# First mixture-of-experts stage of a two-layer decoder: expert weights loaded during the attention in front of it, residual sum of X and normalised X on ScalarE, list products at other places

## The reference

```python
x = x + _L0_xattn_ref(_layernorm(x), ctx_1024, ctx_1024)      # attention in front, "a0"
x = x + _L0_ffn_ref(_layernorm(x), ...)                       # first feed-forward stage, "f0"

def _L0_ffn_ref(x, centroids, routing_bias, Wfc_r, Wproj_r, Wfc_sh, Wproj_sh):   # x is normalised
    raw = einsum('bsd,ed->bse', x, centroids)
    _, top_idx = top_k(sigmoid(raw + routing_bias), 2)         # 2 of 8 routed experts per token
    combine = ...                                              # softmax of the two scores
    shared_out = sum over 2 shared experts of gelu(x @ Wfc_sh.T) @ Wproj_sh.T
    routed_out = sum over 8 experts of combine * (gelu(x @ Wfc_r.T) @ Wproj_r.T)
    return x + shared_out + routed_out
```

## Time and profile before

| what | us |
|---|---|
| median of three runs | 1243.5 (1243.29 to 1244.32) |
| the profiled execution's own time | 1240.97 |
| its span, from the first to the last instruction | 1239.2 |
| PE busy in the span | 1114.3 (90%) |
| DVE busy | 818.9 (66%) |
| ACT busy | 636.0 (51%) |
| POOL busy | 596.2 (48%) |

### The profile page before, as it was taken

How to read it: one execution, slowest core, us unless ns; L and a number is a source line. 1 busy time by engine, 2 the same in 40 slices (tenths; PEclk the granted TensorE clock), 3 DMA queues, 4 the chain that set the end, 5 groups by cost and what they waited for, 6 DMA issues and landing times. The chain is left out here.

```text
span 1239.2 us, 31324 instructions
## 1 busy us (share of the span) xinstructions
PE 1114.3 (90%) x11494; PEld 937.7 (76%) x11494; DVE 818.9 (66%) x1784; ACT 636.0 (51%) x1143; POOL 596.2 (48%) x608
## 2 busy tenths in 40 slices
PE   6989998999999999399999999996899978899970
PEld 4766666679999977288888888885577668899970
DVE  6768997853322443368888888885588867566762
ACT  5416774534566543066666666663678720366640
POOL 4772233315666575634334444442334324677775
PEclk9999998899999999799999999998999969899995
DMA  7001221502233321100000000000011060133342
GB/s 199 10 2 34 71 51 38 208 5 57 69 79 78 91 82 38 40 2 2 0 0 0 0 0 0 0 1 1 19 19 19 8 228 12 53 88 85 86 128 63
DMA packets 59537, 60.78 MB, mean 49 GB/s; under 512 B 12241, under 2 KB 48721, under 8 KB 58929
## 3 DMA queue, kind: packets, MB, share of 16 engines
q1 hardware_dynamic: 49904, 41.63, 11.3%
q0 software_dynamic: 8640, 17.71, 5.6%
q10 hardware_dynamic: 896, 0.17, 0.1%
HBM read 41.77 MB, written 15.60 MB: 46 GB/s over the span
## 5 line engine op out<-in xcount | busy, mean ns | idle before, releaser
L1629 POOL DMA_INDIRECT f_xn<-f_xn_rows,f_source x142 | 138.1, 972 | 41.9 <-issue 40.7
L2012 PE MATMUL f_bank<-f_xT,f_w_tile 128*128 128x128 f32 x1136 | 152.1, 277 | 0.0
L2023 PE MATMUL f_bank<-f_w_down,f_hidden 128*128 x1136 | 150.4, 276 | 0.0
L2012 PEld LDWEIGHTS f_bank<-f_xT,f_w_tile 128*128 128x128 f32 x1136 | 140.5, 194 | 0.0
L2023 PEld LDWEIGHTS f_bank<-f_w_down,f_hidden 128*128 128x128 f32 x1136 | 138.9, 193 | 0.0
L1050 POOL TENSOR_TENSOR ret_rstd<-ret_var,ret_minus_half 128x8 f32<-128x8 f32 x32 | 52.7, 1647 | 173.3 <-DVE ret_var L1089 173.3
L1640 POOL DMA_INDIRECT f_hot_row<-f_slots_y,f_slots x112 | 108.6, 970 | 33.5 <-issue 32.9
L885 PEld LDWEIGHTS a_mixed_psum<-a_v_diag,a_probT 128*64 128x64 f32 x2048 | 66.6, 139 | 59.9 <-ACT a_probT L837 43.7
L747 POOL TENSOR_TENSOR X<-X,a_mixed 128x128 f32<-128x128 f32 x64 | 29.2, 457 | 158.0 <-DVE a_mixed L780 154.6
L1904 ACT ACTIVATE f_w_tile<-f_w_up 128x512 f32 x142 | 87.6, 620 | 28.9 <-DVE f_owner L1809 26.8
L788 DVE TENSOR_REDUCE a_top<-a_scores 128x16 f32<-128x1024 f32 x64 | 78.3, 1224 | 34.2 <-PE a_scores L870 33.3
(11 more groups left out here) (302 smaller groups left out, 2797.5 us busy)
## 6 DMA issues: line engine op xcount, KB each, us to landing
f_slots_y<-f_y_out SPq DMA_DIRECT2D x70, 128.0 KB, 2.3
a_v_rows<-in_ctx SPq DMA_DIRECT2D x16, 256.0 KB, 4.0
f_xn_rows<-f_xn SPq DMA_DIRECT2D x16, 256.0 KB, 13.3
f_w_up<-in_f_up SPq DMA_DIRECT2D x1, 2560.0 KB, 9.8
f_w_down<-in_f_down SPq DMA_DIRECT2D x1, 2560.0 KB, 17.1
f_xn<-f_xn_rows,f_source POOLq DMA_INDIRECT x142, 2.6
X<-in_x SPq DMA_DIRECT2D x4, 512.0 KB, 6.2
kv_ctxT<-in_ctxT SPq DMA_DIRECT2D x8, 256.0 KB, 5.6
```

Of the source, the lines that this page charges most:

```text
L1629: pool.indirect_dma_start(out=x_in[:, s % RING, :], out_offset=None, in_=xn_rows[:, :], in_offset=bass.IndirectOffsetOnAxis(ap=source[:, s ...
L2012: last = pe.matmul(bank_h[m % 3][:, j * P:(j + 1) * P], w_tile[m % W_RING][:, j * P:(j + 1) * P], xT[m % 3][:], start=True, stop=True)
L2023: last = pe.matmul(bank_y[m % 2][:, 0:D].unsqueeze(1), hidden[m % 3][:, j, :], w_down[:, bass.ds(expert + E0, 1), j, :], start=(j == 0), s ...
```

## The change

Three parts, all of them in f0 and the attention a0 in front of it.

1. The weight arrays get a fixed place at the top of SBUF (class `HeldWeights`), and SP starts their two loads as the first instructions of the attention block a0, ahead of a0's own loads of keys and values for the third and later groups. f0 no longer loads them; its engines wait on the new semaphore.
2. POOL's eight additions X + xn are gone. ACT does them, as X * (1 + rstd) + (-mean * rstd), one instruction per tile with a scale and a bias per token, eight tiles after each of the first four shared units. DVE makes the two small operands `x_scale` and `x_shift` behind the last tile of xn. The first gather no longer waits for X + xn, and DVE's additions of shared results count the new semaphore in tiles.
3. The table `COLLECT` puts list products 0 to 4 at other places among the shared units.

```diff
+class HeldWeights:
...
+    def sync(self, sp):
+        for dst, src in ((self.w_up, self.up), (self.w_down, self.down)):
+            sp.dma_start(dst[:], self.g.dram[src]).then_inc(self.loaded, 16)
...
             @block.sync
             def _(sp):
+                if held:
+                    held.sync(sp)
                 for j in range(setup.early, 2):
...
-                if spec["plus_xn"]:
-                    for q in range(GROUPS):
-                        pool.wait_ge(S["xn_ready"], GTILES * (q + 1))
-                        x = g.X[:, GTILES * q:GTILES * (q + 1), :]
-                        pool.tensor_tensor(x, x, xn[:, GTILES * q:GTILES * (q + 1), :], ALU.add)\
-                            .then_inc(S["xn_added"], 1)
...
+                if spec["plus_xn"]:
+                    dve.scalar_tensor_tensor(out=x_shift[:], in0=g.mean[:], scalar=-1.0, in1=g.rstd[:],
+                                             op0=ALU.mult, op1=ALU.mult).then_inc(S["scale_ready"], 1)
+                    dve.tensor_scalar(x_scale[:], g.rstd[:], 1.0, None, ALU.add).then_inc(S["scale_ready"], 1)
...
                     def weights(unit):
+                        if unit < TILES // PLUS_TILES:
+                            act.wait_ge(S["scale_ready"], 2)
+                            act.wait_ge(S["xn_ready"], TILES)
+                            for s in range(PLUS_TILES * unit, PLUS_TILES * (unit + 1)):
+                                nc.scalar.activation(g.X[:, s, :], g.X[:, s, :], ACT.Identity, bias=x_shift[:, s:s + 1],
+                                                     scale=x_scale[:, s:s + 1]).then_inc(S["xn_added"], 1)
...
-                pe.wait_ge(S["weights_loaded"], 16 * len(weight_loads))
+                wait_for_weights(pe)
                 if shared:
-                    COLLECT = {(3, "up"): (0,), (3, "down"): (1,), (4, "up"): (2, 3), (4, "down"): (4, 5),
-                               (5, "up"): (6,), (5, "down"): (7,)}
+                    COLLECT = {(3, "down"): (0, 1), (4, "up"): (2,), (4, "down"): (3, 4)}
```

More of the change, by code:

```diff
@@ L717, in attention @@
         statistics = RowStatistics(g, name, ctx)
+        assert not held or g.nc.sbuf_base <= held.begin
         with nc.Block() as block:
@@ L1457, in ffn_phase @@
         pair, slots = sb("weights", [P, TOP_K, TILES]), sb("slots", [P, TOP_K, TILES], I32)
-        w_up, w_down = sb("w_up", [D, E, FFN]), sb("w_down", [P, E, FT, D])
+        held_weights = spec["held"]
+        if held_weights:
+            w_up, w_down = held_weights.w_up, held_weights.w_down
+        else:
+            w_up, w_down = sb("w_up", [D, E, FFN]), sb("w_down", [P, E, FT, D])
         owner, source = sb("owner", [1, M], I32), sb("source", [P, M], I32)
@@ L1510, in ffn_phase @@
         rows = [h[:].rearrange("p n t d -> p t n d") for h in row_sets]
+        assert not held_weights or nc.sbuf_base <= held_weights.begin
         bank = g.banks(name, ctx)
@@ L1533, in ffn_phase, with wait_for_weights @@
         loads = [(gate_w[:], dram[spec["gate_w"]]), (gate_b[:], dram[spec["gate_b"]].to_broadcast([P, EXPERTS])),
[L1534 removed]
+                 (rank[:], dram["rank"]), (before[:], dram["before"]),
+                 (tile_numbers[:], dram["tile_numbers"]), (segment_table[:], dram["segment_table"]), (row_numbers[:], dram["row_numbers"]),
                  (token_rows[:], dram["token_rows"])]
         n_loads = len(loads)
[L1537 removed]
+        def wait_for_weights(eng):
+            if held_weights:
+                eng.wait_ge(held_weights.loaded, 16 * 2)
+            else:
+                eng.wait_ge(S["weights_loaded"], 16 * len(weight_loads))
+        weight_loads = [] if held_weights else [(w_up[:], dram[spec["w_up"]]), (w_down[:], dram[spec["w_down"]])]
         if biased:
@@ L2033, with ffn0 @@
 WARM_START, WARM_COUNT, WARM_BETWEEN, WARM_UP = 28, 120, 6, 24
-def ffn0(g, weights):
-    ffn_phase(g, "f0", dict(kind="sigmoid", plus_xn=True, part_tiles=(20, 12), last=False, shared=2, following=weights, added_at=(65,), hot_later=(4, 10, 16), listed=16, ahead=(8, 13), more_rows=0, gelu=ACT.Gelu, gate_w="f0_gate_w",
-                            gate_b="L0_ffn_routing_bias", w_up="f0_up", w_down="f0_down", b_up=None))
+def ffn0(g, weights, held):
+    ffn_phase(g, "f0", dict(kind="sigmoid", plus_xn=True, part_tiles=(20, 12), last=False, shared=2, following=weights, held=held, added_at=(65,), hot_later=(4, 10, 16), listed=16, ahead=(8, 13), more_rows=0, gelu=ACT.Gelu, gate_w="f0_gate_w",
+                            gate_b="L0_ffn_routing_bias", b_up=None))
 def ffn1(g):
-    ffn_phase(g, "f1", dict(kind="softmax", plus_xn=False, part_tiles=(16, 8, 8), last=True, shared=0, following=None, added_at=(53, 58, 64, 69), hot_later=(0, 2, 4, 6), listed=8, ahead=(8, 24), more_rows=1, gelu=ACT.Gelu_apprx_tanh,
+    ffn_phase(g, "f1", dict(kind="softmax", plus_xn=False, part_tiles=(16, 8, 8), last=True, shared=0, following=None, held=None, added_at=(53, 58, 64, 69), hot_later=(0, 2, 4, 6), listed=8, ahead=(8, 24), more_rows=1, gelu=ACT.Gelu_apprx_tanh,
                             gate_w="L1_ffn_Wg", gate_b="L1_ffn_bg", w_up="f1_up", w_down="f1_down",
@@ L2050, in layers @@
         g.run(lambda g: ssm_phase(g, setup))
-        g.run(lambda g: attention(g, "a0", setup))
+        held = HeldWeights(g, "f0", 2 + EXPERTS, "f0_up", "f0_down")
+        g.run(lambda g: attention(g, "a0", setup, held))
     with ExitStack() as ctx:
         weights = RetentionWeights(g, ctx)
-        g.run(lambda g: ffn0(g, weights))
+        g.run(lambda g: ffn0(g, weights, held))
         setup = AttentionSetup(g, "a1", True, ctx, early=1)
```

26 lines of the change are left out of this document (17 added, 9 removed).

## The result

The changed kernel takes **1234.1 us** (median of 6 runs, 1230.3 to 1237.2) beside 1242.7 for the kernel before (median of six, the three runs of the opening table among them): ratio 0.9932, 95% interval 0.9919 to 0.9946. So it is faster, by 4.6 to 10.1 us over both intervals. The forecast of 1238.1 had the sign and the mechanism, but was 4 us too slow, and the time lies 1.1 us under its range. The second job's median would lie in the range; how far the whole time was missed is therefore less sure than which terms were missed, and those are read from the profiles. The profiled execution after took 1233.76 us with a span of 1231.9, against 1240.97 and 1239.2: the span is 7.3 us shorter.

The account below looks back on a forecast made before the run. PE, busy 90% of the span, was taken as the bound, losing time ahead of f0's dense part. Gains of 4.6 us (up 0) and 0.8 (clock) make 5.4: 1243.5 - 5.4 = 1238.1 us, range 1235.2 to 1240.7.

Parts of the forecast that it names:

- the mechanism: f0's start: POOL's eight additions stretch xn, xn starves PE and ACT, and PE's lack of work lets the clock fall.
- the weights are needed and worth nothing by themselves: Ahead of up 0: early weights alone remove 0.4 us; without them, logits 4 us sooner would gain nothing.
- the new places gain nothing but keep a loss away: List products among f0's shared units: no gain by itself, but 1 to 3 us kept from being lost.
- the zeros: Cost 0 for ACT's additions in f0's shared units, and 0 for the weight load during a0.
- rival 5: f0's shared units: ACT's additions slow to 0.93 us each and ACT becomes the bound, time 1249.5 us; chance 4%.
- rival 3: a0 pays for the weight load, 2.1 us at the upper bound, time 1240.2 us; chance 8%.
- the clock's term: Around up 0 in f0: slow clock loses 1.7 us in place of 2.5, a gain of 0.8 us.
- So I expect up 0 to begin at 0.50 as now: At up 0 in f0: PE's clock falls to half just before it, as in f1, and returns after 3.4 us.
- rival 1: f0: PE's clock holds at 1.00 through the logits, gain 4.6 + 2.5 = 7.1 us, time 1236.4; chance 21%.
- 4.6 us for up 0: f0: with logits sooner and weights there, up 0 starts at 226.1 in place of 230.67, 4.6 us earlier.
- What starts ACT at 215.58 ... is unchanged: f0's start: warm-up products and table loads stay the same, so ACT's first copy stays at 215.58.
- the 10.52 from f1: f0: bias addition comes 10.52 us behind ACT's first copy, as in f1, in place of 14.70.

Follow-up runs that it names:

- second job: The changed kernel without an edit, measured again beside the kernel before: 1237.1 us against 1243.5, ratio 0.9945.
- p2_undone: Changed kernel with X + xn back on POOL and ACT's additions out, held weights and new list places kept: 1242.4 us, ratio 0.9988 to the kernel before.
- pool_late: Changed kernel with X + xn on POOL, begun only behind the last xn: 1239.2 us, ratio 0.9963 to the kernel before.
- p1_only: Changed kernel with only the early held weights; POOL's additions and the old list places are back: 1242.1 us, ratio 0.999 to the kernel before.
- p1_undone: Changed kernel with f0 loading its own weights at its start again, the other two parts kept: 1243.9 us, ratio 1.0 to the kernel before.
- p3_undone: Changed kernel with the old list places, held weights and ACT's additions kept: 1238.5 us, ratio 0.9967 to the kernel before.
- p3_again: Changed kernel with the old list places, a second profiled execution: 1242.8 us in its one run.
- c_fill: Kernel before with small products in PE's copy-stage waits, 4 per tile from tile 20 on and 6 behind the logits: 1245.2 us, ratio 1.002.
- v_early: Changed kernel with 18 products in place of 28 ahead of f0's copies, PE waiting for the gate weights alone: 1236.8 us, 0.9944 to the kernel before.
- a_same: Changed kernel without an edit, second profiled execution, first of three such repeats: 1237.1 us, ratio 0.9945 to the kernel before.
- a_same3: Changed kernel without an edit, fourth profiled execution: 1235.2 us in one run.
- b_same: Kernel before without an edit, second profiled execution: 1240.8 us in one run.

## Why the prediction was wrong, and where it was right

Right were the mechanism and its sign. PE was held by xn, xn by POOL's additions; p2_undone and pool_late show it from both sides. Right was that the weights are needed and worth nothing by themselves (p1_only, p1_undone), and that the new places gain nothing but keep a loss away (p2_undone, p3_undone, p3_again). That PE's lack of work let the clock fall in the kernel before fits c_fill, where products in those waits held it at 1.00. Right were the zeros: ACT's additions at 481 to 515 ns with no wait of PE for a gelu (rival 5 out), and a0, which takes 118.1 us from its first transpose to f0's first product in both kernels, 91.21 to 209.33 before and 91.74 to 209.82 after, and 118.06 to 118.17 in all 17 profiles, with or without the load in it (rival 3 out).

**The step that failed is the clock's term**: "So I expect up 0 to begin at 0.50 as now", worth 0.8 us. From up 0 to down 0 the profiled execution went from 10.31 to 7.82 us: 2.49, all of what the clock had cost. That is rival 1, to which I gave 21%, and three of four executions took its way; its sum, 7.1 us, was too small as well, by the second term below. I took f1's fall for the rule of a stage with the same pace of work. For f1 it is nearly that. f1 does the same work in all the kernels here (v_early counts one of its loads by a semaphore of its own), and in 14 of the 17 profiles its clock fell before the logits were done, with PE busy without a gap up to the fall; in the other three it fell in the wait behind them. In the changed kernel, the rows on either side of the fall:

```profile
999.04:1002.45 3.41, 3.41 (x35) 3.37 (x34) 0.00 (x0) 3.08 (x12) 0.00 (x0) 1.00 0.96 392
1002.45:1012.69 10.24, 4.11 (x15) 3.58 (x16) 6.96 (x17) 0.51 (x2) 0.00 (x0) 0.50 0.71 255
```

What failed was to carry it over to f0. Eight profiles have f0's copies with xn at its full pace and all 28 products ahead (after, the three a_same, p1_undone, p3_undone, p3_again, pool_late), and the clock fell ahead of the logits' end in two of them, a_same and p3_undone. The instructions in the copies are the same, so they alone do not decide it. By the rule cited from the Trainium skill (TensorE: Matmul & The Clock Gate, "What's actually happening"), that activity releases the throttle, the clock holds; that described three executions and not the fourth. The same section of the Trainium skill calls the moment at which the clock rises run-variable, and the rows below agree (2.9 to 6.0 us); I had not drawn on it.

**A second term was too small: 4.6 us for up 0 measured 5.9** from the stage's first product (21.34 to 15.43). Of the 1.3 us too little, 0.85 lies in "What starts ACT at 215.58 ... is unchanged": the 28 products took 4.92 in place of 6.11 us, since the clock rose 4.2 us after the first of them and not 5.9, and ACT's first copy came 5.40 us in, not 6.25. Copies to bias addition took 10.29 us for the 10.52 from f1, whose end ran at half clock: 0.23. And up 0 begins 0.26 us ahead of the bias addition (225.25 and 225.51), where I had put it at the same time. Two of these three are the clock again, the 0.23 by inference. They are partly the draw of the execution: in a_same, where the clock rose 5.9 us in, as in the profile that the forecast was made from, up 0 came at 16.47, 4.9 us earlier for the forecast's 4.6, and the stretch to down 0 was 1.0 us shorter for its 0.8. That execution is the one that the forecast described, but for a second fall in unit 4.

The books for the two profiled executions: 5.4 forecast + 1.3 (up 0) + 1.7 (clock) + 0.1 (dense part) = 8.5 for the front; 0.5 is lost by f0's later start and 0.7 behind it; 7.3 in the span.

What stays open: why the clock falls in one execution and not in the next. In the six of those eight profiles in which it held through the logits, it had first risen 2.9 to 4.4 us after the stage's first product; in a_same and p3_undone, where it fell ahead of up 0, 5.9 and 6.0. f1 goes the same way: in the 14 profiles with a fall ahead of the logits' end the clock had risen 5.45 to 6.1 us after f1's first product, in the other three (p1_undone, p3_undone, a_same3) 2.7, 5.1 and 5.40. That is what the rows show and no cause; v_early had the rise at 4.2 us and fell in the copies, with 10 products less ahead of them, and b_same had it at 4.4 and fell where PE waited for xn.

## What to carry to other kernels

When an engine off the path runs at a quarter of its pace in the profile, look for another engine that works in the same stretch, and test by moving that work away altogether: moved a little later, it stretched the next thing. Before costing a saving, list what else ends at the same moment; here the logits, the weights and the one-hots stood within a few tenths of a microsecond of where PE needed them, and neither the held weights nor ACT's additions gained anything without the other. A clock's fall in another stage, even one that comes there in 14 of 17 profiles, need not come in yours: give both outcomes a chance in the forecast, and take several profiles of each kernel before pricing it.

## What the runs showed of the hardware that was not expected

- Beside POOL's additions DVE is stretched by operation: a comparison and a multiplication over 128x256 took 1.44 and 1.38 us in place of 0.43, a reduction over 128x256 right behind them 0.42 as ever (pool_late). POOL itself was not slowed: 10.42 us for eight, 1.30 each, against 1.32 beside xn.
- A wait of 2.18 us on PE was followed by two falls of the clock, 1.7 us lost each, in stretches without any idle time (p3_again); with them the front was 5.7 us longer, 2.6 times what the bracket says. Whether the wait had a part in the falls is open.
- The clock fell, and stayed low, while PE was busy: f1's fell to 0.50 in 14 of 17 profiles with PE busy up to the fall (3.41 of 3.41 us in the row from 999.04 above), and in v_early f0's copies and logits ran at 0.50 for 10.79 us with PE busy for 10.79.
- Kernels with one and the same f1 took 242.8 to 246.7 us from its first product to the end of the span (994.75 to 1239.2 before, 986.76 to 1231.9 after), and f0 began between 207.8 and 211.7 us; differences of 2 to 3 us between single executions say nothing about a change.
